# Last norm of a transformer block on one core: small VectorE operations with one operand in PSUM, the root on ScalarE, and a reciprocal with a Newton step on VectorE

## What is computed

```python
def _layer_norm(x, gamma, beta):
    mu = jnp.mean(x, axis=-1, keepdims=True)
    var = jnp.mean((x - mu) ** 2, axis=-1, keepdims=True)
    return (x - mu) * jax.lax.rsqrt(var + EPS) * gamma + beta
...
out = out.reshape(B, S, H) + hidden_states
return _layer_norm(out, gamma, beta)
...
x = x + gb * _L0_ffn_ref(h, ...)
```

## Time and profile before

| what | value |
|---|---|
| time, median of 3 runs | 1345.8 us (1345.49 to 1347.42) |
| time of the profiled execution | 1346.97 us |
| its span, first to last instruction | 1345.2 us |
| busy over the whole span | PE 86%, DVE 74%, ACT 55%, POOL 70% |
| last matrix product in the trace | 1260.32 us |
| last addition on GpSimd | 1326.44 us, 14.70 us for the last 12 of the 32 |

### The profile page before, as it was taken

The page is one execution under the profiler, slowest core; times in us unless marked ns, Lnnn a source line. Parts: engine busy times, 40 slices in busy tenths (PEclk is TensorE's granted clock), DMA queues, the critical chain, the costliest instruction groups (busy, mean ns, idle before and its releaser), DMA issues. The chain is left out here.

```text
span 1345.2 us, 23643 instructions
## 1 busy us (share of the span) xinstructions
PE 1151.3 (86%) x5959; PEld 770.5 (57%) x5960; DVE 990.3 (74%) x2224; ACT 746.1 (55%) x1448; POOL 948.3 (70%) x1086
## 2 busy tenths in 40 slices
PE   7899999999999999999999999999993065989400
PEld 5556566666656566656656566666642045989400
DVE  4888687777777677777777687777675994767596
ACT  4666667666665657666665667565542611444254
POOL 4576978788887969788886969787773205545268
PEclk9899999999999999999999999999995556999755
DMA  5000101010110101020110101010113303233474
GB/s 153 17 19 17 48 18 64 2 64 17 48 47 16 48 16 63 0 63 15 48 47 16 47 16 48 2 49 1 48 48 126 78 1 97 45 95 48 101 251 163
DMA packets 68478, 70.91 MB, mean 53 GB/s; under 512 B 12912, under 2 KB 64032, under 8 KB 68272
## 3 DMA queue, kind: packets, MB, share of 16 engines
q1 hardware_dynamic: 46800, 47.18, 11.0%
q10 hardware_dynamic: 16896, 16.78, 3.7%
q0 software_dynamic: 4704, 6.11, 3.0%
HBM read 40.35 MB, written 29.45 MB: 52 GB/s over the span
## 5 line engine op out<-in xcount | busy, mean ns | idle before, releaser
L705 ACT ACTIVATE PF<-PS 128x512 f32<-128x512 f32 x512 | 298.5, 595 | 256.9 <-PE PS L1087 248.8
L979 DVE TENSOR_REDUCE NMAX<-PS 128x1 f32<-128x512 f32 x512 | 342.5, 682 | 88.5 <-PE PS L1096 85.0
L567 POOL TENSOR_TENSOR SF<-SF,PF 128x512 f32<-128x512 f32 x252 | 323.1, 1303 | 14.0 <-ACT PF L705 13.8
L1168 PE MATMUL PS<-PF,V 128*64 128x512 f32 x1024 | 248.0, 605 | 0.0
L1086 PE MATMUL PS<-Q,K 128*128 128x512 f32 x512 | 221.9, 433 | 2.8 <-ACT PF L705 2.8
L1096 PE MATMUL PS<-K,Q 128*128 128x512 f32 x512 | 205.7, 403 | 10.4 <-DVE NMAX L979 10.2
L1087 PE MATMUL PS<-Q,K 128*128 128x512 f32 x512 | 201.5, 394 | 0.0
L724 ACT ACTIVATE Q<-PS 64x512 fp32r<-64x512 f32 x256 | 151.7, 593 | 48.2 <-PE PS L172 43.3
L644 POOL TENSOR_TENSOR XL<-XF,XH 128x512 fp32r<-128x512 f32 x63 | 83.1, 1320 | 128.2 <-ACT XH L779 128.2
L1086 PEld LDWEIGHTS PS<-Q,K 128*128 128x128 f32 x512 | 96.4, 188 | 120.3 <-issue 55.2
L564 POOL TENSOR_TENSOR SF<-PF 128x512 f32<-128x512 f32 x126 | 162.4, 1305 | 3.9 <-ACT PF L705 3.4
(11 more groups left out here) (351 smaller groups left out, 2449.3 us busy)
## 6 DMA issues: line engine op xcount, KB each, us to landing
X<-in_L_attn_x SPq DMA_DIRECT2D x16, 512.0 KB, 3.5
MODB<-mod_rows SPq DMA_DIRECT2D x16, 512.0 KB, 3.7
h_rows<-H ACTq DMA_DIRECT2D x16, 512.0 KB, 3.0
acc_rows<-H ACTq DMA_DIRECT2D x16, 512.0 KB, 4.1
out_x<-X SPq DMA_DIRECT2D x16, 512.0 KB, 2.9
A<-acc_rows SPq DMA_DIRECT2D x15, 512.0 KB, 8.9
W1F<-in_L_ffn_W SPq DMA_DIRECT2D x3, 1024.0 KB
W2F<-in_L_ffn_W SPq DMA_DIRECT2D x3, 1024.0 KB, 7.4
```

The lines of the kernel that those rows point to most:

```text
L567: s_sum.done(pool.tensor_tensor(total, total, tile, ALU.add))
L705: s_exp.done(act.activation(PF[:, u % 8, :], st_bank(u), ACT.Exp))
L979: s_mred.done(dve.tensor_reduce(NMAX[:, p % 2, r:r + 1], mx_bank(u), AX.X, ALU.max, negate=True))
L1168: last = pe.matmul(num_bank(p)[odd * R:(odd + 1) * R, :], V1[:, vp, c, :], PF[:, k % 8, :], start=(c == 0), stop=(c == TC - 1))
```

## The change

The power on GpSimd, its constant and its semaphore go. ScalarE takes the square root of the variance of each group instead (`ROOT`, function `root`), and VectorE takes the reciprocal of it (step 8) and does a Newton step on that (steps 9 to 11). The tiles `TMP`, `SUM` and three new ones (`ODD`, `DEL2`, `Y2`) become parts of the eighth PSUM bank, and only seven banks are left for the pairs. The steps are reworked so that none has two tensor inputs in SBUF: the odd means are first copied to PSUM (step 0), the difference of the means is formed twice, once into SBUF and once into PSUM, and so on. There are 13 steps for a group where there were ten; eight of them end with the variance.

```diff
--- before.py
+++ after.py
@@ -1862,15 +1862,15 @@
     X1, PS, GBG, s_gbg = m["X1"], m["PS"], m["GBG"], m["s_gbg"]
     GROUPS = (2, 4, 4, 4, 2)
     FIRST = [sum(GROUPS[:j]) * TC for j in range(len(GROUPS) + 1)]
-    STEPS, VAR_DONE, PAIRS, BANKS = 10, 6, NCH // 2, 8
+    STEPS, VAR_DONE, PAIRS, BANKS = 13, 8, NCH // 2, 7
     A = sb("A", [P, NCH, D])
     S6 = sb("S6", [P, NCH, 6])
-    VAR, DEL, SUM, Y, TMP, NMR = (sb(x, [P, NCH]) for x in ("VAR", "DELt", "SUMt", "Yr", "TMP", "NMR"))
-    GATE, HALF = sb("GATEt", [P, NB]), sb("HALFt", [P, NCH])
-
-    s_half = sem("thalf")
+    VAR, DEL, Y, NMR = (sb(x, [P, NCH]) for x in ("VAR", "DELt", "Yr", "NMR"))
+    TMP, ODD, DEL2, SUM, Y2 = (PS[:, BANKS, j * NCH:(j + 1) * NCH] for j in range(5))
+    GATE, ROOT = sb("GATEt", [P, NB]), sb("ROOTt", [P, NCH])
+
     s_in, s_first = [sem(f"tin{b}") for b in range(NB)], [sem(f"tfirst{c}") for c in range(TC)]
-    s_pow, s_gate, s_stat, s_step, s_xn, s_mul, s_add, s_out = (sem(x) for x in ("tpow", "tgate", "tstat", "tstep", "txn", "tmul", "tadd", "tout"))
+    s_root, s_gate, s_stat, s_step, s_xn, s_mul, s_add, s_out = (sem(x) for x in ("troot", "tgate", "tstat", "tstep", "txn", "tmul", "tadd", "tout"))
     acc_rows = m["acc_dram"][0:NT, :].rearrange("(c p) n -> p c n", p=P)
     out_rows = out.rearrange("b (c p) n -> p (b c) n", p=P)
 
@@ -1911,36 +1911,50 @@
 
 
             cols = slice(FIRST[j], FIRST[j + 1])
-            v, d, t, y, s, nmr = (x[:, cols] for x in (VAR, DEL, TMP, Y, SUM, NMR))
+            v, d, t, y, s, nmr, odd, d2, y2 = (x[:, cols] for x in (VAR, DEL, TMP, Y, SUM, NMR, ODD, DEL2, Y2))
             mean_e, m2_e, mean_o, m2_o = (S6[:, cols, i] for i in (1, 2, 4, 5))
+
+            def made(i):
+
+                dve.wait_ge(s_step, STEPS * j + i + 1)
+
             if k == 0:
                 dve.wait_ge(s_stat, FIRST[j + 1])
-                dve.tensor_scalar(t, m2_e, 1.0 / D, EPS, ALU.mult, ALU.add).then_inc(s_step, 1)
+                ins = dve.tensor_copy(odd, mean_o)
             elif k == 1:
-                dve.tensor_tensor(d, mean_e, mean_o, ALU.subtract).then_inc(s_step, 1)
+                ins = dve.tensor_scalar(t, m2_e, 1.0 / D, EPS, ALU.mult, ALU.add)
             elif k == 2:
-                dve.wait_ge(s_step, STEPS * j + 1)
-                dve.scalar_tensor_tensor(out=v, in0=m2_o, scalar=1.0 / D, in1=t, op0=ALU.mult, op1=ALU.add).then_inc(s_step, 1)
+                made(0)
+                ins = dve.tensor_tensor(d, mean_e, odd, ALU.subtract)
             elif k == 3:
-                dve.wait_ge(s_step, STEPS * j + 3)
-                dve.tensor_tensor(t, d, d, ALU.mult).then_inc(s_step, 1)
+                ins = dve.tensor_tensor(d2, mean_e, odd, ALU.subtract)
             elif k == 4:
-                dve.tensor_tensor(s, mean_e, mean_o, ALU.add).then_inc(s_step, 1)
+                made(1)
+                ins = dve.scalar_tensor_tensor(out=v, in0=m2_o, scalar=1.0 / D, in1=t, op0=ALU.mult, op1=ALU.add)
             elif k == 5:
-                dve.wait_ge(s_step, STEPS * j + 4)
-                dve.scalar_tensor_tensor(out=v, in0=t, scalar=0.25, in1=v, op0=ALU.mult, op1=ALU.add).then_inc(s_step, 1)
+                made(3)
+                ins = dve.scalar_tensor_tensor(out=d2, in0=d2, scalar=0.25, in1=d, op0=ALU.mult, op1=ALU.mult)
             elif k == 6:
-                dve.wait_ge(s_pow, j + 1)
-                dve.tensor_tensor(t, y, y, ALU.mult).then_inc(s_step, 1)
+                ins = dve.tensor_tensor(s, mean_e, odd, ALU.add)
             elif k == 7:
-                dve.wait_ge(s_step, STEPS * j + 7)
-                dve.scalar_tensor_tensor(out=t, in0=t, scalar=-0.5, in1=v, op0=ALU.mult, op1=ALU.mult).then_inc(s_step, 1)
+                made(5)
+                ins = dve.tensor_tensor(v, d2, v, ALU.add)
             elif k == 8:
-                dve.wait_ge(s_step, STEPS * j + 8)
-                dve.scalar_tensor_tensor(out=y, in0=t, scalar=1.5, in1=y, op0=ALU.add, op1=ALU.mult).then_inc(s_step, 1)
+                dve.wait_ge(s_root, j + 1)
+                ins = dve.reciprocal(y2, ROOT[:, cols])
             elif k == 9:
-                dve.wait_ge(s_step, STEPS * j + 9)
-                dve.scalar_tensor_tensor(out=nmr, in0=s, scalar=-0.5, in1=y, op0=ALU.mult, op1=ALU.mult).then_inc(s_step, 1)
+                made(8)
+                ins = dve.tensor_tensor(d, v, y2, ALU.mult)
+            elif k == 10:
+                made(9)
+                ins = dve.scalar_tensor_tensor(out=d, in0=d, scalar=-0.5, in1=y2, op0=ALU.mult, op1=ALU.mult)
+            elif k == 11:
+                made(10)
+                ins = dve.scalar_tensor_tensor(out=y, in0=d, scalar=1.5, in1=y2, op0=ALU.add, op1=ALU.mult)
+            elif k == 12:
+                made(11)
+                ins = dve.scalar_tensor_tensor(out=nmr, in0=s, scalar=-0.5, in1=y, op0=ALU.mult, op1=ALU.mult)
+            ins.then_inc(s_step, 1)
 
         def scale(q):
 
@@ -1973,9 +1987,18 @@
 
     @block.scalar
     def _(act):
+        def root(j):
+
+            cols = slice(FIRST[j], FIRST[j + 1])
+            act.wait_ge(s_step, STEPS * j + VAR_DONE)
+            act.activation(ROOT[:, cols], VAR[:, cols], ACT.Sqrt).then_inc(s_root, 1)
+
+        root(0)
         for j in range(len(GROUPS)):
             act.wait_ge(s_step, STEPS * (j + 1))
             for c in range(FIRST[j], FIRST[j + 1]):
+                if j + 1 < len(GROUPS) and c == (FIRST[j] + FIRST[j + 1]) // 2:
+                    root(j + 1)
                 if c % 2 == 0 and c // 2 >= BANKS:
                     act.wait_ge(s_mul, c // 2 - BANKS + 1)
                 act.activation(pair_bank(c // 2)[:, c % 2 * D:(c % 2 + 1) * D], A[:, c, :], ACT.Identity,
@@ -1983,20 +2006,7 @@
 
     @block.gpsimd
     def _(pool):
-        pool.memset(HALF[:, :], -0.5).then_inc(s_half, 1)
-        pool.wait_ge(s_half, 1)
-
-        def power(j):
-
-            cols = slice(FIRST[j], FIRST[j + 1])
-            pool.wait_ge(s_step, STEPS * j + VAR_DONE)
-            pool.tensor_tensor(Y[:, cols], VAR[:, cols], HALF[:, cols], ALU.pow).then_inc(s_pow, 1)
-
-        power(0)
         for q in range(PAIRS):
-            for j in range(1, len(GROUPS)):
-                if 2 * q == FIRST[j - 1]:
-                    power(j)
             pool.wait_ge(s_mul, q + 1)
             x = X1[:, 2 * q:2 * q + 2, :]
             pool.tensor_tensor(x, x, A[:, 2 * q:2 * q + 2, :], ALU.add).then_inc(s_add, 1)
```

## The result

The changed kernel takes 1333.11 us (median of 4 runs, 1329.99 to 1333.91) against 1346.61 us before (4 runs, 1345.49 to 1348.48). The ratio is 0.9896 with a 95% interval of 0.9883 to 0.9908, so 13.5 us less. The forecast was 1332.6 us from 1345.8, 13.2 us less.

What follows compares the result with a forecast made beforehand. The bound was taken as VectorE's small SBUF steps waiting for GpSimd's additions, plus GpSimd's powers and idle time. Gains of 4.6 and 8.6 us, together 13.2, gave 1332.6 us; own range 1331 to 1334.5, overall 1330 to 1338.

Steps and rivals of the forecast that it cites:

- First term: Last norm, up to the twelfth VectorE multiply: small steps no longer wait for GpSimd's additions, 4.6 us gained.
- Second term: Last norm, twelfth multiply to the end: GpSimd runs 21 additions without powers or idle time, 8.6 us gained.
- Keeping ahead: Rounds 4 and 5: VectorE needs 8.6 us, ScalarE's bank filling 8.0 us, both under GpSimd's 9.8 us of additions.
- Costs at nothing: Around the last norm: table load, later roots, seven banks, removed constant and output transfers were to add no time.
- Rival A: VectorE's small steps writing PSUM cost as much as the reciprocal row, losing 3.5 us: 1336.1 us; chance 0.10.
- Rival B: VectorE's copy, first scaling and reciprocal, reading SBUF alone, still wait for additions, losing 3.5 us: 1336.1 us; chance 0.12.
- Rival C: In the last norm PSUM operands free nothing and VectorE becomes the bound, 47 steps waiting: 1350.9 us; chance 0.04.

Runs made afterwards that it cites:

- delay_round3: Changed kernel with six extra statistics of a constant tile on VectorE in round 3, one in each of slots 5 to 10; 1336.06 us.
- delay_round5: Changed kernel with six extra statistics on VectorE in the last three slots of round 5, two in each; 1333.72 us.
- scratch_in_sbuf: Changed kernel with its five scratch tiles in SBUF instead of PSUM, root still on ScalarE; 1347.64 us, ratio 1.0004 to the kernel before.
- step_kinds: Changed kernel with small extra VectorE instructions (copies, scalings, reciprocals, a product; SBUF or PSUM operands) beside GpSimd's additions in rounds 4 and 5; 1334.06 us.
- power_kept: Changed kernel with PSUM operands, but GpSimd's power kept and copied to PSUM instead of ScalarE's root and the reciprocal; 1343.34 us, ratio 0.9968 to the kernel before.
- root_alone: Kernel before with ScalarE's root and VectorE's reciprocal replacing the power, 11 steps a group, all scratch in SBUF; 1345.62 us, ratio 0.9983.

## Why the prediction was right

- *First term, up to the twelfth multiply, forecast 4.6 us.* The first multiply comes 9.51 us after the fifth statistic instead of 9.29 (1273.89 us before, 1270.45 after): 0.2 us where I had 0.4. From the first multiply to the end of the twelfth it is 1298.34 - 1279.96 = 18.4 us instead of 23.6; I had 18.6. So the term is 5.2 - 0.2 = 5.0 us. The 0.08 us for a step holds in PSUM too, and is 0.06 to 0.07 for the 128x8 ones, which is the small rest.
- *Second term, forecast 8.6 us.* From the twelfth multiply's end 25.8 us (predicted 25.7) instead of 34.3: 8.5 us. delay_round3 and delay_round5 show that VectorE is the bound before this stretch and GpSimd late in it. The two terms together are 13.5 us, the measured difference.
- *Keeping ahead.* VectorE waits 2.5 us in all for ScalarE's banks in rounds 5 and 6, and ends 4.6 us before GpSimd; the prediction's rounds (8.6 and 8.0 us against 9.8) gave a slack of that size.
- *Costs at nothing.* Table load, roots, seven banks and the output transfers: nothing of them is in the chain. One reading behind this was wrong: I took every later root's variance to be ready when ScalarE is half through a group, and ScalarE waited 1.23 and 0.45 us for two of them. It was hidden, since VectorE waited for no bank before 1307.85 us.
- *Rival A* (PSUM dear): its price is up to 20 ns in a duration, and none between starts. The higher fixed cost of a PSUM source that the Trainium skill gives ("VectorE: DVE Perf Modes", the TRN2 errata) does not show here: 16-element steps with a PSUM source took 156 to 182 ns, undisturbed ones between SBUF tiles 155 to 169 (scratch_in_sbuf).
- *Rival B* (one-source steps still wait): L1923 and L1925, SBUF to PSUM, take 174 and 175 ns; step_kinds shows that a copy and a scaling wait when both sides lie in SBUF. The PSUM side frees them.
- *Rival C* is refuted for the change, but scratch_in_sbuf is its kernel: it ended even, not at 1350.9 us. The wait I used for its price, 0.55 us for each of 47 steps, is 25.9 us. Measured were 17.0 us, or 0.36 us a step: the mechanism of the estimate was right, and the term that failed is the share of steps that are blocked. Additions that starve block less, as the prediction said, but it took off too little for it: GpSimd stood idle 16.7 us there (3.5 us in the change), and 27 of the 47 steps did not wait.
- *A misread row.* The prediction calls both small steps of the earlier trace rows 128x8. The one at 1317.93 us (L1943) belongs to group 3 and works on 16 elements. Nothing in the sum depends on it.

What the prediction did not say is what each half of the change is worth, and its two terms are not these halves: they are two stretches of time. power_kept and root_alone fill this in. PSUM alone shortens the first stretch from 23.6 to 18.8 us and leaves the second at 34.5. Root alone leaves the first at 24.8 us and takes the second from 34.3 to 31.7 only. So nearly all of the first term comes from the PSUM operands, and the second, 8.5 us, needs both. In root_alone VectorE's waits fill most of the place of the powers: behind the twelfth multiply GpSimd lost 6.9 us before to two powers and the idle time in front of them, and it loses 5.6 us there to waits for multiplies.

## What to carry to other kernels

When a VectorE instruction of 0.15 us lasts as long as whatever GpSimd is doing, look at where its operands lie: one side in PSUM was enough here, at up to 20 ns a step. Take away both halves of such a coupling together: here each half alone gave 4.7 and 1.5 us of 13.8, because the engine that was freed alone waited for the other. And measure a short stage between two marks inside it, since the stages ahead moved by 6 us from one profile to the next while the changed kernel's stage repeated within 0.01 us in the two profiles of it.

## What the runs showed of the hardware

- A copy of 15 or 16 elements from SBUF to SBUF took up to 1.23 us beside GpSimd's additions, as long as a product of two SBUF sources. A reciprocal between the same tiles took 0.19 to 0.24 us. I had left the reciprocal open; why it differs is not settled by these runs.
- A small copy, scaling or two-source step between SBUF tiles waited only for an addition in progress. In scratch_in_sbuf L1930, right behind L1928, took 169 ns, since GpSimd had nothing to add then; with additions queued, L1950 took 1.19 us although L1947 right in front of it had just waited 0.5 us. That only 20 of 47 steps waited is why my count of blocked steps was too high.
- GpSimd's additions do not lengthen for it: 1258 to 1274 ns each before, and means of 1267 ns in the change, 1262 in scratch_in_sbuf and 1264 in root_alone. Only VectorE's instructions became longer.
